# Two graph layers on one core: dense cells that fetch a row per edge and sum by a second product

## What is computed

```python
h = relu(layernorm(x))
m_data = h[src] @ W_data.T + b_data ; m_ctrl = h[src] @ W_control.T + b_control
msg = where(edge_types == 0, m_data, m_ctrl)
x = x + relu(segment_sum(msg, dst) + h @ W_self.T + b_self)            # layer 0
h = relu(layernorm(x))
g = tanh((h @ gate_w[:, :D])[dst] + (h @ gate_w[:, D:])[src] + gate_b)
yn = tanh(edge_weight * yes_weight + (1 - edge_weight) * no_weight)
e = (g + yn) * 0.5 * deg_isqrt[dst] * deg_isqrt[src]
x = x + segment_sum(h[src] * e, dst)                                   # layer 1
```

## Time and profile before

| | |
|---|---|
| median of three runs | 6028.04 us |
| profiled execution, its span | 6027.32 us, 6025.2 us |
| TensorE busy, mean granted clock | 4934.1 us (82%), 0.907 |
| VectorE busy | 4823.0 us (80%) |
| ScalarE busy | 4476.2 us (74%) |
| GpSimd busy | 4422.1 us (73%), 4134.6 of it in 4320 of the loops' gathers |
| DMA queues of SP and of GpSimd | 29.1% and 20.2% of 16 engines |

### The profile page before, as it was taken

The page is one execution under the profiler, slowest core; times in us unless marked ns, Lnnn a source line. Parts: engine busy times, 40 slices in busy tenths (PEclk is TensorE's granted clock), DMA queues, the critical chain, the costliest instruction groups (busy, mean ns, idle before and its releaser), DMA issues.

```text
span 6025.2 us, 135015 instructions
## 1 busy us (share of the span) xinstructions
PE 4934.1 (82%) x35643; PEld 3849.3 (64%) x35643; DVE 4823.0 (80%) x19569; ACT 4476.2 (74%) x13367; POOL 4422.1 (73%) x4589
## 2 busy tenths in 40 slices
PE   6588888888888888888378888888888888888884
PEld 5466666666666666676356666666666666666664
DVE  6877777777777778775378888888888888888884
ACT  5878888888888888873167778787787777877770
POOL 5777777777777777777737777777777777777774
PEclk8599999999999999998588899899898898989895
DMA  7756666666666666666353333333333333333334
GB/s 239 252 169 176 174 175 175 175 175 174 174 175 175 175 175 172 177 173 191 95 155 93 94 94 95 96 94 97 94 93 94 97 94 93 97 93 94 94 91 118
DMA packets 407112, 833.79 MB, mean 138 GB/s; under 512 B 95935, under 2 KB 188131, under 8 KB 405859
## 3 DMA queue, kind: packets, MB, share of 16 engines
q1 hardware_dynamic: 256387, 520.84, 29.1%
q0 software_dynamic: 144896, 301.67, 20.2%
q10 hardware_dynamic: 5088, 2.64, 0.2%
HBM read 764.42 MB, written 60.37 MB: 137 GB/s over the span
## 4 chain that ended last, share of the span: by engine, by line
PE 40%; DVE 23%; ACT 15%; issue 13%; POOL 5%; DMA 2%; DVEq 1%; SPq 1%; ACTq 0%; POOLq 0%
PE PS L805 15%; PE PS L972 8%; PE PS L835 6%; POOL G L520 5%; DVE OHF L1596 5%; PE PS L824 3%; ACT OHF L657 3%; PE PS L962 3%; ACT PAY L636 3%; DVE OHF L1598 2%; DVE OHF L1518 2%; ACT PAY L637 2%; DVE OHF L1507 2%; DVE OHF L1587 1%; ACT PAY L638 1%
## 5 line engine op out<-in xcount | busy, mean ns | idle before, releaser
L520 POOL DMA_INDIRECT G<-t,IDX x4320 | 4134.6, 957 | 1368.5 <-issue 1310.3
L657 ACT ACTIVATE OHF<-PS 128x512 bf16<-128x512 f32 x1568 | 896.6, 587 | 554.3 <-PE PS L824 542.9
L1596 DVE TENSOR_TENSOR OHF<-HTB,PS 128x256 f32<-128x256 f32 x1568 | 649.6, 414 | 185.5 <-PE PS L972 182.8
L972 PE MATMUL PS<-OHF,HTB 128*128 128x256 f32 x1568 | 576.1, 453 | 193.8 <-DVE OHF L1598 182.2
L805 PE MATMUL PS<-OWF,G 128*128 128x32 f32 x4528 | 616.9, 294 | 139.5 <-DVE OWF L1548 80.8
L972 PE MATMUL PS<-OHF,CDST 128*128 128x256 f32 x1568 | 572.7, 451 | 176.6 <-DVE OHF L1598 167.9
L805 PEld LDWEIGHTS PS<-OWF,G 128*128 128x128 f32 x4528 | 608.3, 216 | 160.0 <-DVE OWF L1548 96.2
L1598 DVE TENSOR_TENSOR OHF<-OHF,PS 128x256 f32<-128x256 f32 x1568 | 659.7, 421 | 53.6
L805 PE MATMUL PS<-OHF,G 128*128 128x32 f32 x4528 | 584.9, 286 | 120.7 <-DMA G<-t,IDXB 55.4
L805 PEld LDWEIGHTS PS<-OHF,G 128*128 128x128 f32 x4528 | 579.7, 208 | 129.0 <-issue 101.8
L835 PE MATMUL PS<-OHF,HTB 128*128 128x256 bf16 x4704 | 650.4, 275 | 0.0
(11 more groups left out here) (253 smaller groups left out, 11551.2 us busy)
## 6 DMA issues: line engine op xcount, KB each, us to landing
HTB<-t0s SPq DMA_DIRECT2D x392, 384.0 KB
OWF<-t0s SPq DMA_DIRECT2D x392, 384.0 KB
G<-t,IDX POOLq DMA_INDIRECT x4320
HTB<-t SPq DMA_DIRECT2D x112, 462.0 KB
CDST<-t SPq DMA_DIRECT2D x112, 462.0 KB
t0s<-HTB SPq DMA_DIRECT2D x25, 384.0 KB
t0s<-OWF SPq DMA_DIRECT2D x24, 384.0 KB
t<-G SPq DMA_DIRECT2D x14, 462.0 KB, 3.5
```

The costliest lines, as they stand in the source:

```text
L520: eng.indirect_dma_start(out=G[:, k:k + width], out_offset=None, in_=table, in_offset=bass.IndirectOffsetOnAxis(ap=at, axis=0)).then_inc(s ...
L657: eng.activation(CA[:, k % 4, :], PS[:, 2 + k % 2, :], ACT.Identity).then_inc(q_ev, 1)
L972: eng.matmul(PS[:, 4 + g % 2, 0:DW], TC1[c % 2][:, b % CB, 0:D], CA1[:, k % 2, :], start=b == 0, stop=b == NB - 1).then_inc(d_ap, 1)
L1596: eng.tensor_tensor(CA1[:, k % 2, :], TG1[:, k % 3, :], PS[:, bank, 0:DW], ALU.mult).then_inc(d_m, 1)
```

## The change

- **Groups.** 16 groups of 62 tiles and two of 60, DT = 1112 (GBEG, GROUP, place_of); 251 items. The groups' first targets come as a new input g0. AHEAD is 6 for 3.
- **Layer 0, cell.** Instead of the count matrix, a one-hot of the source's row (transposed: rows of the block x edges) fetches for each edge its row from the block (gather), ScalarE copies the 384 columns of three bf16 parts (evacuate), and apply sums them by a one-hot of the target, 256 wide. For the transposed one-hot the edges' codes must lie along the free axis: turn_codes transposes them, code_rows writes them as int16, ScalarE sends them to DRAM (rows), and SP loads them for each pair, broadcast to all partitions, before the pair's parts. pair_hots makes both types' one-hots of a pair.
- **Sort.** The payload is two fp32 values, 1024 x target + code and the weight, in one fp32 product; convert prepares the first from int16 copies. The splitting of weights in bf16 parts goes (split, the last two lines of payload, two products of place). The place is one tile later.
- **Layer 1, cell.** pair_hots1 and gather1 fetch 129 columns per edge in fp32; target_score picks the target's gate part by a comparison with accumulated product; ScalarE adds the gate, the weight and scales the copied rows (gate1, weight1, evacuate1); apply1 sums by an fp32 one-hot of the target. combine, pieces, gates and cell_table go. SP loads two blocks at a time in a ring of four; a slot is freed by the gather.
- **Counts.** The reduction over four one-hots becomes two additions.

```diff
-GT = 60
-NG = 16
+RUNS = ((16, 62), (2, 60))
@@ sync
-                    eng.wait_ge(q_ap, (c - RT + 1) * HB)
+                    eng.wait_ge(q_ga, (c - RT + 1) * HB)
+                if part == 0:
+                    eng.wait_ge(q_rs, 16 * (g + 1))
+                code_rows(RB0[:, c % RT, :], g, 0, part, q_tc[c % RT])
...
@@ scalar
-                hot, to, rest = OHB[:, t % KO, :], PAY[:, t % 3, :], PAYR[t % 3]
-                eng.activation(to[:, 0:NB], hot, ACT.Identity, scale=S1F[:, t:t + 1])
-                eng.activation(to[:, NB:2 * NB], hot, ACT.Identity, scale=S2F[:, t:t + 1])
-                eng.activation(to[:, 2 * NB:TW], hot, ACT.Identity, scale=YG[g % 2][:, 0, j:j + 1])
-                eng.activation(rest[:, 0:NB], hot, ACT.Identity, scale=YG[g % 2][:, 1, j:j + 1])
-                eng.activation(rest[:, NB:2 * NB], hot, ACT.Identity,
-                               scale=YG[g % 2][:, 2, j:j + 1]).then_inc(q_p, 1)
+                hot, to = OHB[:, t % KO, :], PAY[:, t % KP, :]
+                eng.activation(to[:, 0:NB], hot, ACT.Identity, scale=CV[:, g % 2, 1, j:j + 1])
+                eng.activation(to[:, NB:PW], hot, ACT.Identity, scale=YG[:, g % 2, j:j + 1]).then_inc(q_p, 1)
...
+                eng.activation(TH1[:, k % KW1:k % KW1 + 1], cell_slot(k)[:, D:D + 1], ACT.Tanh,
+                               bias=PDE[:, g % 2, b:b + 1]).then_inc(d_th, 1)
+                eng.activation(WV1[:, n:n + 1], TH1[:, n:n + 1], ACT.Identity,
+                               bias=TABS[:, g % 2, PW + b:PW + b + 1]).then_inc(d_w, 1)
+                eng.activation(X1[k % KX1], cell_slot(k)[:, 0:D], ACT.Identity, scale=WV1[:, n:n + 1]).then_inc(d_ev, 1)
@@ tensor
-                eng.matmul(PS[:, 2 + k % 2, :], CSRC[:, k % KB, :], CDST[:, k % KB, :], start=True, stop=True)\
-                   .then_inc(q_a, 1)
+                for t in range(2):
+                    ins = eng.matmul(PS[:, cell_bank(k), 0:384].rearrange("p (n w) -> p n w", n=3),
+                                     OT0[c % 3][:, t, col:col + 128], TC[c % RT][:, k % HB, :, t * D:(t + 1) * D],
+                                     start=t == 0, stop=t == 1)
+                ins.then_inc(q_ga, 1)
...
-                for h in range(2):
-                    for n in range(3):
-                        ins = eng.matmul(PS[:, 4, 0:DW], TC[c % RT][:, b % HB, n, h * D:(h + 1) * D],
-                                         CA[:, k % 4, h * DW:(h + 1) * DW],
+                for n in range(3):
+                    ins = eng.matmul(PS[:, 4, 0:DW], X0[:, k % KX, n, :], CD0[:, k % KD, :],
...
-                eng.matmul(PS[:, 7, 0:TW], OHR[:, t % KR, :], PAY[:, t % 3, :], start=t % GT == 0, stop=False)
-                eng.matmul(PS[:, 7, 2 * NB:TW], OHR[:, t % KR, :], PAYR[t % 3][:, 0:NB], start=False, stop=False)
-                eng.matmul(PS[:, 7, 2 * NB:TW], OHR[:, t % KR, :], PAYR[t % 3][:, NB:2 * NB],
-                           start=False, stop=last).then_inc(q_tab, 1)
+                eng.matmul(PS[:, 7, 0:PW], OHR[:, t % KR, :], PAY[:, t % KP, :],
+                           start=j == 0, stop=j == SIZE[g] - 1).then_inc(q_tab, 1)
...
+                eng.matmul(cell_slot(k), OT1[c % RT][:, col:col + 128], TC1[c % RT][:, k % HB, 0:D + 1],
+                           start=True, stop=True).then_inc(d_ga, 1)
+                eng.matmul(PS[:, 4 + g % 2, 0:DW], X1[k % KX1], CD1[k % KD1],
+                           start=b == 0, stop=b == NB - 1).then_inc(d_ap, 1)
@@ vector
+            def pair_hots(c):
+                eng.wait_ge(q_tc[c % RT], parts_in(c))
+                if c >= 3:
+                    eng.wait_ge(q_ga, HB * (c - 2))
+                for t in range(2):
+                    ins = eng.tensor_scalar(OT0[c % 3][:, t, :], RB0[:, c % RT, :], PCODE[:, t:t + 1], None,
+                                            ALU.is_equal)
+                ins.then_inc(q_ot, 1)
...
-                eng.tensor_scalar(CSRC[:, k % KB, :], IOS[:, :], TABS[:, g % 2, b:b + 1], None, ALU.is_equal)
-                eng.tensor_scalar(CDST[:, k % KB, :], IO16[:, :], TABS[:, g % 2, NB + b:NB + b + 1], None,
+                eng.tensor_scalar(CD0[:, k % KD, :], IO16[:, 0:DW], TABS[:, g % 2, NB + b:NB + b + 1], None,
                                   ALU.is_equal).then_inc(q_oh, 1)
...
+                eng.scalar_tensor_tensor(JUNK[k % 2], IO16[:, 0:DW], TABS[:, g % 2, NB + b:NB + b + 1],
+                                         ACC[:, 1, bass.ds(start1[0], DW)], ALU.is_equal, ALU.mult,
+                                         accum_out=PDE[:, g % 2, b:b + 1]).then_inc(d_pd, 1)
...
+            def cell1(k):
+                if k % HB == 0 and k + 2 * HB < NG * NB:
+                    pair_hots1(k // HB + 2)
+                if k + 3 < NG * NB:
+                    target_score(k + 3)
+                if k >= 1:
+                    cell_hots1(k - 1)
```

More of the change, by code:

```diff
@@ L25 @@
 NC = NB // CB
-GT = 60
-NG = 16
-DT = NG * GT
+RUNS = ((16, 62), (2, 60))
+SIZE = [n for count, n in RUNS for _ in range(count)]
+NG = len(SIZE)
+GBEG = [sum(SIZE[:g]) for g in range(NG + 1)]
+DT = GBEG[NG]
+GT = max(SIZE)
+GROUP = [g for g in range(NG) for _ in range(SIZE[g])]
 DW = 256
@@ L50 @@
 RT = 4
[L51 to L52 removed]
+USTEP = 15
+KO, KU, KR, KH, KP = 8, 5, 4, 4, 4
+KD, KX = 8, 4
+KD1, KX1, KW1 = 6, 6, 8
+PACK = 1024
 def spread(total, parts):
@@ L60, in plan @@
 def plan():
-    ends = [0, 16]
+    ends = [0, 17]
     rest = SM - ends[1]
@@ L385, in _, with code_rows @@
                 eng.wait_ge(q_tc[n], 16 * units(n))
+            def code_rows(to, g, n, part, s):
+                row = rows[g, n, part * HB:(part + 1) * HB, :].rearrange("b r -> (b r)")
+                eng.dma_start(to, row.unsqueeze(0).broadcast_to([128, HB * 128])).then_inc(s, 16)
             for c in range(NG * NH):
@@ L444, in _ @@
                     table(1)
-                if part == 3 and 1 <= g < NG - 1:
+                if part == 10 and 1 <= g < NG - 1:
+                    eng.wait_ge(d_ap, g * NB)
                     eng.wait_ge(d_tb, 16 * (g + 1))
@@ L866, in _ @@
                     if k < CELL[s + 1]:
-                        build(k)
-                        if k >= 2:
-                            apply(k - 2)
+                        gather(k)
+                        if k >= LATE:
+                            apply(k - LATE)
                     if t < TILE[s + 1]:
-                        if t >= LAG + 1:
-                            place(t - LAG - 1)
+                        if t >= LAG + 2:
+                            place(t - LAG - 2)
                         ranks(t)
                 if s == LASTT:
-                    for t in range(DT - LAG - 1, DT):
+                    for t in range(DT - LAG - 2, DT):
                         place(t)
@@ L984, in _ @@
                 tiles_into(1, s % 2, s, OW[:, s % 2, :, :]).then_inc(e_pe, 1)
-            for k in range(NG * NB - APPLY, NG * NB):
+            for k in range(NG * NB - LATE1, NG * NB):
                 apply1(k)
@@ L1641, in _ @@
                     first_section(1)
-            for k in range(NG * NB - COMB, NG * NB):
-                combine(k)
+            cell_hots1(NG * NB - 1)
             adds1(SM - 1, done)
@@ L1689 @@
         "d0": starts,
+        "g0": whole(np.asarray(inputs["dst"])[:GBEG[NG] * 128:128][GBEG[:NG]][None, :], (128, NG)),
         "typ": edges("edge_type_2", 0),
```

493 lines of the change are left out of this document (267 added, 226 removed).

## The result

The changed kernel takes 5919.99 us (median of four runs, 5918.08 to 5921.97) where the kernel before, timed beside it, takes 6027.56 (6025.36 to 6028.04): ratio 0.982, 95% interval 0.9805 to 0.9839. It is faster by 107 us, 1.8%. Forecast were 254, with a range of 5640 to 5900 that the result misses by 20.

The account below looks back on a forecast made before the run. The gather queue was taken to pace both loops, with VectorE becoming layer 0's bound after the change. 6027.3 us - 83 (layer 0) - 171 (layer 1) = 5773 us; range 5690 to 5900, with the fast case 5640 to 5900.

Parts of the forecast that it names:

- The bound and what is removed: Both loops: the gather queue sets the pace, 10.06 us an item; 152 gathers less a layer save 191 us each.
- TensorE, ScalarE: Layer 0: TensorE goes from 8.3 to 8.8 us an item, not the bound; ScalarE falls clear of the bound.
- the signs written down: Layer 0: GpSimd waits for TensorE 0.5 to 0.7 us an item, VectorE over 90% busy, ScalarE under 65%.
- Layer 0, VectorE: Layer 0: VectorE becomes the bound at 10.7 us an item, ends 10.4 and 11.2; layer 0 changes by -83 us.
- the 30 us taken off it: Layer 0: five slots absorb about three items, 30 us of VectorE's 138, given back in the last 19 items.
- The item's own part: Layer 0, VectorE: hots, counts, adds, register loads and group decoding per item, 2.73 us after the change, 2.6 before.
- Layer 1: Layer 1: VectorE's 9.6 us an item stays under the gathers' 10.06; -191 us less 20 for stretched gathers gives -171.
- The stretch: Layer 1: VectorE instructions with both inputs in SBUF lengthen gathers, 0 to 62 us, 20 taken.
- Around the loops: Outside the loops, with sort setup, edge weights, transfers and added waits: zero, 5 us at most.
- Layer 1 doesn't gain: Layer 1: slow fp32 one-hots or score-stretched gathers (0.7 us an item) leave 0 to -20; total 5930; chance 0.09.
- Layer 0 is heavier: Layer 0: VectorE takes 11.2 us an item, so +24 with layer 1 at -171; total 5880; chance 0.14.
- The ring of four pairs: Pair loads, hidden at load time L of 4 to 5 us, become the bound from L = 5.9; slower, chance 0.06.

Follow-up runs that it names:

- The kernel at the old size: Changed kernel's new form of cells, payload and pairs with 16 groups of 60 dense tiles, 270 items: 6102.1 us, layer 0 2735.4, layer 1 2785.1.
- the last one: Changed kernel with layer 1's score and target comparison reading numbers from PSUM, two register lists, rank's one-hot on ScalarE: 5735.3 us, ratio 0.9525 to the kernel before.
- the kernel with two lists: Changed kernel with separate VectorE register lists for addresses of items' own edges and of extra items: 5870.2 us, layer 0 2671.4.

## Why the prediction was wrong

**The bound and what is removed: right.** The gathers pace both loops of the kernel before, at 10.06 us an item; each layer lost 191 us of them. The kernel at the old size, and layer 1 of the last one, come to the same 1.26 us a gather.

**TensorE, ScalarE: right, with a reserve.** Cutting TensorE's work gained nothing in layer 0 (at a lower clock), and it waits for VectorE there; ScalarE fell to 57% busy. Of the signs written down, GpSimd's wait for TensorE came, with 1.1 us an item for 0.5 to 0.7, but VectorE is 85% busy there and not over 90%: the waits below don't count as busy.

**Layer 0, VectorE: the mechanism right, the size off.** Forecast was -83 us, measured -7. The step that failed is the sum of 10.7 us an item, and the 30 us taken off it. From item 30 to 232 an item takes 10.97 us, within the ends of 10.4 to 11.2. By the mean spacing of starts from 1000 to 2000 us a cell's two comparisons were 0.42 for the 0.45 taken and a tile step 0.94 for 0.96; that is 0.32 us an item to the good. The item's own part was 3.3 for 2.73. Two terms were missing in it. The extra items were costed by their hot, count and adds, without the reload of eight addresses at each change to them and back; the kernel with two lists prices that at 0.27 us. And the waits for loaded pairs stood at nothing, "hidden", by a rule for the average; they are 0.25 us an item. 10.70 - 0.32 + 0.27 + 0.25 = 10.90 of 10.97. (10.97 - 10.70) x 202 items = 55 us. The other 20 are the discount of 30: items 17 to 30 still went at 10.10 us, which is worth some 11, but the first 17 stood at 10.71, as they did before the change (10.83), and the last 18 gave nothing back and stood at 10.44.

**Layer 1: the right mechanism at a quarter of its size.** Forecast -171, measured -111. VectorE is paced by the gathers there (79% busy), as the sum of 9.6 us has it. The stretch was written down with 0 to 62 us, and 20 taken, "since most such meet no gather at the wrong moment". It was 80. Of the 2008 gathers 653 start inside a score. The score's part, 44 us, lay within the range; taking a third of it on a guess about meetings was the first error, since a row that groups the gathers (the 0.953 of the earlier trace rows) can't tell how many meet such an instruction in a kernel that has far more of them. The second is that the comparison was not on the list: it has one wide input in SBUF and was costed by its length alone, and its 26 us are outside any range that I gave. In the earlier trace rows comparisons are queued behind L1507 while the gather takes its 1.09 us, and I put all of that on L1507. Of the remaining 10 us no run takes anything apart; by the table above the pair's hot (L1663, which also reads SBUF and writes fp32) has some 7, 200 gathers at 0.035.

The Trainium skill (SBUF — State Buffer, "Who interferes with whom") has two kinds of VectorE instruction that contend with GpSimd: those with two SBUF inputs, and single-source ones such as a comparison with a scalar when they run in a mode that uses both port pairs; a PSUM operand rules these modes out (VectorE: DVE Perf Modes, "Mode 2×_2P — use both read ports for one tensor" and "Why PSUM operands drop a tier"). The prediction drew on the first kind only. The runs bear out both: 44 us for an input of the score, 26 for the input of the comparison, which from PSUM takes 0.479 us for 0.361, as one that has left a faster mode would; the mode itself stands in no trace. The blocking of the second to start, which the prediction cites, fits the counts by the gather's start.

**Around the loops:** 11 us for the 5 at most that were written down.

**The rivals.** "Layer 1 doesn't gain" had the stretch at its full size, 0.7 us an item; it is 0.32. "Layer 0 is heavier" had 11.2 us an item for 10.97. The result lies between the forecast and these two: they were drawn as alternatives, but a bit of both came at once, and the range ended at the single worst of each. The ring of four pairs, the slower rival, did not decide; but VectorE waited 0.25 us an item for it, and 1.3 once it was lighter (how much of that the loop paid is not shown), so it stood nearer than "from L = 5.9" said.

## What to carry to other kernels

When a change trades work on a full queue against work on an engine with some slack, sum that engine's item in start-to-start spacings and put every small wait into the sum, register loads and loads from the ring as well: where the slack is 10%, they decide. An instruction that is hidden in time can still cost its neighbour: before adding one per cell, list all that read a wide operand from SBUF, comparisons with a scalar included, and count in a trace how many gathers start inside one. Where VectorE has room, a constant operand in PSUM frees the gathers even though the comparison itself becomes slower.
